# State-space gates: where the pool engine begins a pair's products and sums

## What is computed

```python
def _bi_wkv(r, k, v, w, u, time_emb):
    tf = sigmoid(sum(time_emb, -1))
    decay = exp(-exp(w)) * (0.5 + 0.5 * tf)
    ek = exp(minimum(k, 30.0))
    ekv = ek * v
    # forward and backward over the tokens: a = a * decay + ekv ; b = b * decay + ek
    nf, df = scan(forward)
    nb, db = scan(backward)
    euk = exp(minimum(u + k, 30.0))
    num = nf + nb - ekv + euk * v
    den = df + db - ek + euk
    return sigmoid(r) * (num / maximum(den, 1e-08)) * (0.8 + 0.2 * tf)

x = x + mamba2(_bi_wkv(x, side, side, ...))            # layer 0: state-space mixer
x = x + moe(_bi_wkv(x, side, side, ...))               # layer 0: 8 experts, top 2
x = x + attention(_bi_wkv(x, side, side, ...))         # layer 1: 16 heads, 4 groups, causal
x = x + gated_mlp(_bi_wkv(x, side, side, ...))         # layer 1
```

## Time and profile before

| | |
|---|---|
| Median of 3 runs | 2657.7 us (2655.0 to 2658.5) |
| Profiled execution | 2656.0 us, its span 2654.3 us |
| TensorE busy (matmul) | 2254.9 us, 85% |
| VectorE busy | 1921.7 us, 72% |
| ScalarE busy | 933.3 us, 35% |
| Pool engine busy | 682.5 us, 26% |
| Granted TensorE clock, mean | 0.93 of full speed |

### The profile page before, as it was taken

The page is one execution under the profiler, slowest core; times in us unless marked ns, Lnnn a source line. Parts: engine busy times, 40 slices in busy tenths (PEclk is TensorE's granted clock), DMA queues, the critical chain, the costliest instruction groups (busy, mean ns, idle before and its releaser), DMA issues.

```text
span 2654.3 us, 32921 instructions
## 1 busy us (share of the span) xinstructions
PE 2254.9 (85%) x10143; PEld 1698.7 (64%) x10160; DVE 1921.7 (72%) x2901; ACT 933.3 (35%) x1910; POOL 682.5 (26%) x545
## 2 busy tenths in 40 slices
PE   0788979978885699988846889999999998999998
PEld 0344444443445578767635777887887877788886
DVE  8898888889885865666645557787787776566665
ACT  2252342342432232333322334444444444322222
POOL 5433434334341434333221002212212210000000
PEclk9899989989985899989967889999999999899999
DMA  5000001001023332343141000001001101000001
GB/s 200 16 32 32 32 16 48 16 25 39 32 79 125 136 112 65 111 150 111 48 162 41 24 16 32 32 0 40 32 0 40 48 16 57 31 24 24 24 12 63
DMA packets 50501, 142.17 MB, mean 54 GB/s; under 512 B 4768, under 2 KB 4768, under 8 KB 46064
## 3 DMA queue, kind: packets, MB, share of 16 engines
q1 hardware_dynamic: 31872, 89.89, 9.5%
q10 hardware_dynamic: 12864, 32.81, 3.3%
q0 software_dynamic: 5680, 18.62, 2.4%
HBM read 106.95 MB, written 34.34 MB: 53 GB/s over the span
## 4 chain that ended last, share of the span: by engine, by line
PE 42%; issue 29%; POOL 9%; DVE 9%; POOLq 5%; ACT 3%; DMA 1%; ACTq 1%; SPq 0%; DVEq 0%
PE bank L341 9%; PE bank L342 9%; PE bank L343 9%; PE bank L2211 4%; PE bank L2212 4%; PE bank L2213 4%; PE bank L2174 3%; POOLq L491 2%; POOL g_v L492 2%; POOL g_v L499 2%; POOLq L517 1%; DVE mw L1716 1%; PE bank L2206 1%; POOLq L514 1%; POOLq L503 1%
## 5 line engine op out<-in xcount | busy, mean ns | idle before, releaser
L2048 PE MATMUL bank<-um,w_in 128*128 128x512 f32 x576 | 260.6, 606 | 7.3 <-DVE lm L1440 7.1
L2048 PEld LDWEIGHTS bank<-um,w_in 128*128 128x128 f32 x576 | 108.9, 194 | 137.2 <-issue 125.7
L341 PE MATMUL bank<-u_hi,aw_hi 128*128 (+1 forms) x384 | 158.7, 413 | 9.4 <-issue 9.4
L1077 ACT ACTIVATE probs<-bank,nmx 128x128 f32<-128x128 f32 (+3 forms) x256 | 131.8, 528 | 90.8 <-DVE nmx L1837 90.8
L343 PE MATMUL bank<-u_hi,aw_lo 128*128 (+1 forms) x384 | 152.3, 397 | 0.0
L342 PE MATMUL bank<-u_lo,aw_hi 128*128 (+1 forms) x384 | 152.2, 396 | 0.0
L1084 ACT ACTIVATE pt_hi<-bank 128x512 fp32r<-128x512 f32 (+1 forms) x192 | 93.9, 526 | 161.1 <-PE bank L2174 161.1
L341 PE MATMUL bank<-u_hi,fw_hi 128*128 128x512 f32 x352 | 136.9, 389 | 0.0
L342 PE MATMUL bank<-u_lo,fw_hi 128*128 128x512 f32 x352 | 136.9, 389 | 0.0
L343 PE MATMUL bank<-u_hi,fw_lo 128*128 128x512 f32 x352 | 136.9, 389 | 0.0
L2174 PE MATMUL bank<-ident,probs 128*128 128x128 f32 x640 | 97.1, 285 | 46.3 <-DVE pt_lo L1852 26.4
(11 more groups left out here) (380 smaller groups left out, 6238.4 us busy)
## 6 DMA issues: line engine op xcount, KB each, us to landing
m_stage<-in_moe SPq DMA_DIRECT2D x21, 1024.0 KB, 6.3
y_slot<-m_o ACTq DMA_DIRECT2D x39, 256.0 KB, 2.5
g_v<-in_fT SPq DMA_DIRECT2D x18, 512.0 KB, 3.4
gates<-g_v SPq DMA_DIRECT2D x18, 512.0 KB, 2.8
f_stage<-in_ffn SPq DMA_DIRECT2D x11, 768.0 KB, 4.4
u_g<-gates SPq DMA_DIRECT2D x8, 1024.0 KB, 5.6
aw_in<-in_att SPq DMA_DIRECT2D x4, 1280.0 KB, 6.2
w_in<-in_w_in ACTq DMA_DIRECT2D x1, 4640.0 KB, 16.8
```

The source lines that it names most:

```text
L341: nc.tensor.matmul(out, hi_w, hi_x, start=start, stop=False)
L1077: A(probs[:, h % 2, PR_AT[qb]:PR_AT[qb] + w], S_[bk][:, c0:c0 + w], ACT.Exp, bias=nmx[:, h % 2, qb:qb + 1], scale=SCALE, accum_out=rsum[:, ...
L2048: mm = M(dst[:], w_in[:, k, c0:c0 + P], um[:, k, :], start=(k == 0), stop=(k == KC - 1))
```

## The change

`gate_products` and `gate_add` get a parameter `both`. With it, the products of either tile wait until all four clamps of the pair are done (`g_clamped` at k * 4 + 4, instead of k * 4 + 2 for tile 0), and the sums of either tile until all scans of the pair are done (`V_SUMS[1]`, 10, instead of `V_SUMS[0]`, 5, for tile 0). For tile 1 nothing changes. `pair_gate` passes `both=True`: this is 17 pairs of the state-space stage and three of attention. The other callers keep their waits. No instruction, buffer or transfer is added or removed, and no order on any engine changes.

```diff
-        def gate_products(eng, k, s, t):
+        def gate_products(eng, k, s, t, both=False):
             v, e, ek, eu = g_tile(s, t)
             mult = nc.gpsimd.tensor_tensor
-            eng.wait_ge(g_clamped, k * 4 + (2 * t + 2))
+            eng.wait_ge(g_clamped, k * 4 + (4 if both else 2 * t + 2))
             mult(e, ek, v, ALU.mult)
             eng.drain()
             mult(v, eu, v, ALU.mult).then_inc(g_pool, 1)

-        def gate_add(eng, k, s, t):
+        def gate_add(eng, k, s, t, both=False):

             v, e, ek, eu = g_tile(s, t)
-            eng.wait_ge(g_vec, k * V_PAIR + V_SUMS[t])
+            eng.wait_ge(g_vec, k * V_PAIR + V_SUMS[1 if both else t])
             nc.gpsimd.tensor_tensor(eu, eu, ek, ALU.add).then_inc(g_pool, 1)
             nc.gpsimd.tensor_tensor(v, v, e, ALU.add).then_inc(g_pool, 1)

@@ in pair_gate
                 for t in range(2):
-                    gate_products(pool, k, s, t)
+                    gate_products(pool, k, s, t, True)
                 for t in range(2):
-                    gate_add(pool, k, s, t)
+                    gate_add(pool, k, s, t, True)
```

## The result

The changed kernel takes 2668.4 us (median of 6 runs, 2667.0 to 2671.8) against 2658.1 for the kernel before on the same chip (6 runs, 2653.1 to 2662.5): ratio 1.004, 95% interval 1.0029 to 1.0051, so 10.3 us slower. The forecast was 2669.6 us, 11.9 above before. The profiled execution of after is the longest of its six, 2671.8 us (span 2670.1), and that of before lay 2.1 us under its median; between these two traces stand 15.8 us, 5.5 more than between the medians.

What follows compares the result with a forecast made beforehand. VectorE's order was taken to mostly bound the state-space stage, TensorE's attention. State-space +8.1 and attention +3.8 us made +11.9; 2656.0 + 11.9 + 1.7 (profiled run to median) = 2669.6 us, range 2658 to 2676.

Steps and rivals of the forecast that it cites:

- Softplus chain: First pair of each sequence: two 64-column steps no longer meet tile 0's products, about 1.9 us gained, 7.6 in four sequences.
- First scan of the first pair: First scan waits 0.6 us for the product train, tile 1's scans gain 0.3: +0.3 us net, +1.2 over four.
- Second pair: Clamps lose their collision but the next taps wait for ScalarE: nothing gained; train reaches first scan, +0.4 us over four.
- Third pair, products: Four-product train delays a two-input step 1.1 us and the first scan 1.05: +2.15 us there, 7.3 over four sequences.
- Third pair, sums: Four sums behind all scans meet one more two-input step, +1.1 us less the following wait: +1.5 us over four sequences.
- Fourth pair: Clamp and tile 1's scans shorten, input product and denominator wait: +0.55 us three times, +0.7 last, +2.35 in all.
- The very first pair: Before the loop: first scans meet two products (+2.2), later scans get free (-1.8), denominator waits for sums (+2.5): +2.9 us.
- Attention: Second pair of three trips: normalisation meets two products, +1.75 us, and a 0.47 us TensorE gap goes: +3.8 us in all.
- (a): Rival: removed waits count, new ones don't, in third pair and normalisation; -15 us, 2642.7 us; chance 0.07.
- (b): Rival: slack further on takes most of the third pair's and attention's losses; +3 us, 2661 us; chance 0.15.
- (c): Rival: margins fail in second pair and attention; denominators wait for last sum or a product goes twice; 2675 us; chance 0.15.
- (d): Rival: the change does nothing, the pool engine being late anyway; 2657.7 us; chance 0.03.

Runs made afterwards that it cites:

- the control: Kernel before with every wait unchanged, only the pool engine's loop rewritten (very first pair apart, then one trip per sequence): 2653.5 us.
- the extra products: Two unused pool products per pass added to the control: behind the third pair's products 2657.9 us, behind the second pair's sums 2654.2 us.
- the whole change in the new loop: All waits of the change, in the pool engine's loop as rewritten for the control: 2667.5 us, +14.0 against the control.
- the kernel without the third pair's products: Whole change in the control's loop, but the third pair of each pass keeps its products' waits as before: 2656.7 us, +3.2 against the control.

## Why the prediction was right, and where its steps were off

The sum was near: 11.9 forecast, 10.3 by the medians. The mechanism holds in the rows of every part, but the agreement of the sum is in part luck: in the traces the parts come to less than forecast, and waits that the forecast did not have stand beside them. Part by part:

- **Softplus chain**, -1.9 a sequence: the shift falls by 1.9 in each of the four (1.93 in the first, 1.90 and 1.91 in the others). Right, place and size.
- **First scan of the first pair**, +0.3 net with the sum that leaves tile 1's scans: the shift grows by 0.1 to 0.2 to the split of csT. The denominators wait longer and the wait for a tap behind them shrinks from 3.37 to 1.83 us: the cover held.
- **Second pair**, nothing gained at the clamps: right, for the reason given; the 1.95 us gap shows it.
- **Third pair, products**, 7.3: 1.41, 1.62, 2.17 and 1.40, together 6.6. The size is near, but of the 2.17 in the third sequence, where 2.15 was forecast, 0.76 is a wait for TensorE ahead of the steps (L1539, absent there in before); the meetings alone cost 1.4 to 1.6 in each sequence. The place is partly wrong, and by the prediction's own sign ("wrong if the third pair's scans stay at 1.21") this step failed: I had the first step unharmed and the first scan hit; the scans stayed at their own length, and the two steps ahead of them took both meetings. The replay was some tenths of a microsecond off, and each meeting still found some two-input step.
- **Third pair, sums**, 1.5: the meetings cost 0.93 each and the wait for TensorE gave back 0.81, 1.20 and 0.93 in three sequences, 0.4 net with small changes between. Together the third pair stands at 7.0 in the traces for 8.8 forecast; it is the term that is most too large.
- **Fourth pair**, +0.55 three times and +0.7: 0.4 and 0.5. The scans ended 1.2 us earlier and the input product and the denominators took 1.6 back, 1.9 in the last sequence.
- **The very first pair**, +2.9: 2.7.
- **Attention**, +3.8: 4.0 by medians, 3.5 in the trace. The parts were each too small: products cost 1.86 a trip for 1.75, and moving the sums gave 0.70 for 0.47, 1.24 in the last trip.

The state-space stage comes to +7.7 for +8.1, but not by these parts: they make 4.3, and the other 3.4 are a wait for TensorE of 1.7 us in the first and in the second sequence that the forecast had no term for (it is taken up below). With attention's 3.5 to 4.0 the forecast's own terms measure 7.8 to 8.3 us where it had 11.9. The first pair and the second pair's first scan (+0.7 for +1.6), the third pair and the fourth are each too large, and that wait fills most of the gap.

The forecast had no term for the expert stage either, where the trace of after gains 4.5 us more. The change does not touch the waits there, but VectorE meets the pool engine's products at other moments: three weight-split steps (L1716) take 10.37 us together for 7.79 in before. The traces of the other kernels stand there between 2.0 less and 2.3 more than before, whether or not they have the change's products, so this part is not shown to belong to the change, and the 15.8 us between the profiled executions are not all effect. Nor do the parts explain the medians to the end: the kernel with attention as before stands 10.0 above the control, where the parts above make 4.3 + 2.0 = 6.3; the two traces, with that wait and the expert stage in them, differ by 11.3.

Of the rivals, (a) had the sign wrong: two of the removed waits did count, and the new ones met their two-input steps nearly every time. (b), that slack takes the loss, is real but small: the wait behind the third pair, 3 us in four sequences, could be used once; the sums' term held it already. (c) did not come: the margins held in the second pair and in attention. (d) is out: the two softplus steps of the earlier trace rows fell to 0.22 and 0.20 us.

The rule of the Trainium skill ("SBUF — State Buffer", section "Who interferes with whom") that a VectorE instruction with at most one SBUF input outside the two-port modes is not concerned agrees with the unchanged lengths and the 0.7 us of the extra products among steps that read PSUM, against 4.4 among two-input steps.

**What stays open.** The third pair's products cost 10.8 us by medians and 6.6 in the traces of before and after. A wait of 1.7 us at L1458 for TensorE may be the rest. It was there in two of four sequences in before, and in all four in after. Two stretches of VectorE's timeline, first sequence, before and then after:

```profile
164.24 0.56 DVE L1458 TENSOR_TENSOR state<-bank,dt 128x384 f32<-128x384 f32 x1
```

```profile
166.84 0.56 DVE L1458 TENSOR_TENSOR state<-bank,dt 128x384 f32<-128x384 f32 x1 [1.78 <-PE bank L2077]
```

and the clock in the same stretches (columns as in the earlier trace rows), again before, then after:

```profile
158.00:165.00 7.00, 4.59 (x20) 2.39 (x18) 6.85 (x13) 3.75 (x5) 2.77 (x3) 1.00 0.01 2
```

```profile
159.00:168.00 9.00, 6.22 (x19) 2.88 (x18) 7.15 (x14) 3.75 (x5) 5.11 (x5) 0.81 0.01 2
```

Where the granted clock was 2.4 GHz throughout there is no wait; where part of the stretch ran at 1.2 GHz (mean 0.81) there is. This holds in all 13 traces of this case: in 28 of their 52 sequences VectorE waits 1.4 to 1.8 us there, and the granted clock over the 6 us up to the step is 0.72 to 0.77; in the other 24 it waits at most 0.23 and the clock is 1.00.

How often it comes goes some way with the change. It came in 16 of 20 sequences of the five kernels that have a train of four at the third pair (after, the whole change in the new loop, attention as before, products alone, the extra products there), and in 12 of 32 of the others. The whole change in the loop of the control had it in three sequences, the kernel without the third pair's products in one: 2 x 1.7 = 3.4 us of the 8.7 by which their state-space stages differ. But each kernel has one trace, in the 8 us ahead of the two stretches TensorE was busy throughout in either kernel, the wait stands ahead of the third pair in its own sequence, and the runs of one kernel spread over 5 to 12 us. Whether the change makes the low clock more frequent, or it fell so by chance, was not tried. The same holds for the 2.5 of the 4.5 us between before and control that the softplus chain leaves.

## What to carry to other kernels

When a helper engine's instructions are gathered into a train, list what stands beside the train's new place, instruction by instruction, rather than what it leaves: here the same products cost 11 us in one pair and paid 5 in another. A busy time that falls (the scans, -3.8 us) is a gain only if the idle time ahead of the group does not rise by more. And before a variant is compared, run it once with its edit off: the rewritten loop alone was worth 4.5 us, beside an effect of 10.3.

## What the runs showed of the hardware that I had not expected

- An order of starts at the scale of 0.1 us decides a whole meeting: with the pool engine's product 0.36 us behind the clamp a 64-column step takes 1.26 us, at 0.49 us it takes 0.23, and the next ones share the loss (0.86 and 0.82 for 1.06 and 0.23). The loop's end on the pool engine makes that difference.
- The pool engine loses as well when it comes second: its last sum, issued 0.6 us into VectorE's input product of 2.78 us, took 3.32 us (1.26 and 1.27 for its neighbours), so it waited for that instruction to end.
- The runs of the kernel before spread over 9 to 11 us, as wide as the change's effect; what can be told from a single profiled execution is where instructions meet, not what the total is.
